# Second attention: who bounds the logarithms of the last two of eight tiles

## The chip, the cores and the metric

The kernel runs on one core of a Trainium2 chip. The metric is the device time of one execution in microseconds (us); lower is better. Engines are named as in the profile: PE is TensorE (PEld its weight loads), DVE is VectorE, ACT is ScalarE, POOL is GpSimd, SP is SyncE.

## The reference, cut to what matters

The whole reference is a chain of a first attention, a mixture-of-experts feed-forward, a second attention and the same feed-forward again, over 4 batches of 1024 tokens of 256 features. The change lies in the second attention, which weighs by inverse squared distance and has no softmax:

```python
sq = q2 + swapaxes(k2, -1, -2) - 2.0 * einsum('bhqd,bhkd->bhqk', Q, K)
dist = sqrt(maximum(sq, 0.0))
W = (SHEP_EPS + dist) ** (-2)
W = W / (SHEP_EPS + sum(W, axis=-1, keepdims=True))
A = einsum('bhqk,bhkd->bhqd', W, V)          # then O = (G * A) @ W_out + X
```

It has 16 heads of 16 features, over two layernorms (the layer's own, and the one in front of it).

## The kernel before, in words

`attention_b` takes the heads in groups of four. Four batches times four groups are 16 units, and each unit is done in two halves of 512 queries: 32 periods, numbered j. In a period the weights are held as `w`, 8 tiles of 128 keys by 4 heads by 512 queries, so one tile (`one(m)`) is 128x2048 f32. Every tile goes through the same steps, each on another engine:

- PE multiplies keys by queries into a ring of three slots (L1951, "dist"); a tile has two slots' worth, one per pair of heads.
- ACT takes the logarithm of both (L1867, in `log`), which writes `w`, and signals `s_log` (L1869). The first time that a tile is rewritten it waits until the old one was used (`s_pv`).
- DVE bounds the logarithm from below by `LOG_MIN`, in place (L1770, in `bound`), and signals `s_bound`.
- ACT takes the sigmoid of minus half of it (L1909), in place, behind a wait on `s_bound`.
- DVE squares it (L1827), in place, and signals `s_wts`.
- PE multiplies values by weights (L1939, "values") into `acc`, and signals `s_pv`.

The sigmoid and the logarithm need different tables, so ACT works in two phases: all eight sigmoids of period j, a table load (L1917), all sixteen logarithms of period j + 1, a table load (L1906). DVE's program follows it: the gates of period j - 1 (L1786 to L1791), eight squares of period j with small work between them, then eight bounds of period j + 1. Each engine has its own queue, written out by hand as a loop over j, and executes it in order; PE's comes from a list (`ORDER`).

The small work of DVE between the squares is, in even periods, the next unit's queries, keys and values (`take`, L1737 to L1744) and their lengths (`lengths`, L1754 and L1757), in odd periods the copies of four transposed operands (`operand`, L1764). Between the bounds, behind bound 3, stands the layernorm of the next batch, three times in a batch: in its second period the first moments (L1708 to L1713), in its third the first normalisation and the second moments, in its fourth the second normalisation (L1723). The last batch has none.

GpSimd has little to do here. In each period it builds two of a unit's four stacks (`build`, L1663 to L1669): in even periods it waits for the lengths, in odd ones for the operand that was copied from the same buffer (`s_qkT`). PE transposes the stacks (L1984), and DVE's `operand` copies them. In the second and third period of a batch it takes the layernorm's root (L1640), and in the third, ahead of that, it makes the next batch's residual with two additions over 128x2048 (L1646 and L1648), as soon as DVE has normalised (`s_x1`). The wait for that is at L1645; the root behind it is needed by DVE one period later.

The change adds a semaphore and a helper to GpSimd, shortens both loops that call `bound` (L1818 and L1838 of the profile's numbering, around `bound(0, m)` and `bound(j + 1, m)`), and changes the wait of the sigmoid at L1908. The functions it touches:

Of the kernel before, what the change touches and what calls it, by code (L numbers as in the profile page):

```python
# [26 lines left out]
TB = L // P  # L27
# [91 lines left out]
def attention_a(nc, c, X, W, sem):  # L119
# [15 lines left out]
    LOWEST = -3.0e38  # L135
    STACKS = [(e, i) for e in range(PAIRS) for i in range(2)]

# [105 lines left out]
    with ExitStack() as ctx:  # L243
# [100 lines left out]
        with nc.Block() as block:  # L344
# [169 lines left out]
            def _(act):  # L514
# [3 lines left out]
                for step in ORDER:  # L518
# [35 lines left out]
                    elif what == "stack":  # L554

                        u, i = step[1:]
                        e, side = STACKS[i]
                        s.copy((kT if side else qT)[:, u % 3, e, :], src).then_inc(s_act, 1)
# [29 lines left out]
            def _(pe):  # L588
                ident = c["ident"]
                pe.wait_ge(s_init, 1)  # L590
                for step in ORDER:
# [37 lines left out]
                    elif what == "stack":  # L629

                        u, i = step[1:]
                        e, side = STACKS[i]
                        pe.wait_ge(s_built, 2 * u + side + 1)
# [855 lines left out]
def attention_b(nc, c, X, x, W, sem):  # L1489
# [7 lines left out]
    UNITS = B * NG  # L1497
    PERIODS = 2 * UNITS
    LOG_MIN = -64.0 * math.log(2.0)
    STACKS = [(e, i) for e in range(PAIRS) for i in range(2)]  # L1500

    def moved(j):
# [5 lines left out]
        if j % 2 and (j + 1) // 2 < UNITS:  # L1508
            out += [("stack", (j + 1) // 2, i) for i in range(len(STACKS))]
        if p == 4 and b + 1 < B:  # L1510
# [5 lines left out]
    def first():  # L1516

        out = [("tokens", 0, x) for x in range(2)] + [("qkv", 0, x) for x in range(2)]
        out += [("stack", 0, i) for i in range(len(STACKS))]
        return out + [("dist", 0, m) for m in range(TB)]  # L1520
# [29 lines left out]
    with ExitStack() as ctx:  # L1550
# [44 lines left out]
        s_qkT = sem("b_stack_transposed")  # L1595
        s_log = sem("b_log_distances")
        s_bound = sem("b_log_distances_bounded")
        s_sig = sem("b_root_weights")
        s_wts = sem("b_weights_ready")
        s_pv = sem("b_weights_used")  # L1600
# [8 lines left out]
        def one(m):  # L1609
            return w[:, m].rearrange("p h n -> p (h n)")  # L1610
# [8 lines left out]
        with nc.Block() as block:  # L1619
# [14 lines left out]
            @block.gpsimd  # L1634
            def _(pool):

                def root(n):

                    pool.wait_ge(s_var, n + 1)
                    pool.tensor_tensor(rstd[:], vpe[:], c["half"][:, 0:TB], ALU.pow).then_inc(s_rstd, 1)  # L1640

                def residual(b):

                    xs = X[:, b * TB:(b + 1) * TB, :]
                    pool.wait_ge(s_x1, b + 1)  # L1645
                    pool.tensor_tensor(xs, xs, xn[:], ALU.add)  # L1646
                    pool.drain()
                    pool.tensor_tensor(xs, xs, b_out[:].unsqueeze(1).to_broadcast([P, TB, D]), ALU.add)  # L1648
                    pool.drain().then_inc(s_xadd, 1)

                def build(n, i):

                    e, side = STACKS[i]
                    heads = slice(2 * e, 2 * e + 2)
                    src = qk[:, :, heads, side, :]
                    norm = len2[:, :, heads, side:side + 1]
                    st = (ks if side else qs)[:].rearrange("p t (h n) -> p t h n", h=2)
                    hi2, lo, at = (DH, 2 * DH, 3 * DH + 2) if side else (2 * DH, DH, 3 * DH)
                    pool.wait_ge(s_len, 2 * n + 2)
                    if n or e:  # L1660

                        pool.wait_ge(s_qkT, len(STACKS) * n + i - 1)
                    pool.tensor_copy(st[:, :, :, 0:DH].bitcast(F32R), src)  # L1663
                    pool.tensor_copy(st[:, :, :, hi2:hi2 + DH].bitcast(F32R), src)
                    pool.tensor_copy(st[:, :, :, at:at + 1].bitcast(F32R), norm)
                    pool.drain()
                    pool.tensor_tensor(st[:, :, :, lo:lo + DH], src, st[:, :, :, 0:DH], ALU.subtract)
                    pool.tensor_tensor(st[:, :, :, at + 1:at + 2], norm, st[:, :, :, at:at + 1], ALU.subtract)
                    pool.drain().then_inc(s_stack, 1)  # L1669

                pool.memset(vg[:], 0.0)
                pool.memset(qs[:], 0.0)
                pool.memset(ks[:], 0.0)
                pool.drain()
                for h in range(2):
                    pool.memset(qs[:, :, h * KC + 3 * DH + 2:h * KC + 3 * DH + 4], 1.0)
                    pool.memset(ks[:, :, h * KC + 3 * DH:h * KC + 3 * DH + 2], 1.0)
                pool.memset(vg[:, :, :, :, DH:DH + 1], 1.0)
                pool.drain().then_inc(s_init, 1)
                root(0)  # L1680
                pool.wait_ge(s_w, WLOADS)
                residual(0)
                root(1)
                for i in range(len(STACKS)):
                    build(0, i)
                for j in range(PERIODS):
                    b, p = divmod(j, TB)
                    n = j // 2 + 1
                    for i in range(2):
                        if n < UNITS:  # L1690
                            build(n, 2 * (j % 2) + i)
                    if b + 1 < B:
                        if p == 1:
                            root(2 * b + 2)
                        if p == 2:
                            residual(b + 1)
                            root(2 * b + 3)

            @block.vector
            def _(dve):  # L1700
# [58 lines left out]
                def operand(n, i):  # L1759

                    at = AT["stack", n, i]
                    e, side = STACKS[i]
                    R.wait_ready(dve, at, ())
                    v.tensor_copy((kT if side else qT)[:, n % 2, e, :], slot(at)).then_inc(R.free[at % SLOTS], 1)  # L1764
                    dve.drain().then_inc(s_qkT, 1)

                def bound(j, m):

                    dve.wait_ge(s_log, TB * j + m + 1)
                    v.tensor_scalar(one(m), one(m), LOG_MIN, None, ALU.max).then_inc(s_bound, 1)  # L1770

# [43 lines left out]
                    lengths(0, x)  # L1815
                for i in range(len(STACKS)):
                    operand(0, i)
                for m in range(TB):  # L1818
                    bound(0, m)
                for j in range(PERIODS):  # L1820
                    b, p = divmod(j, TB)
                    if j:
                        gates(j - 1)
                    n = j // 2 + 1
                    for m in range(TB):
                        dve.wait_ge(s_sig, TB * j + m + 1)
                        v.tensor_tensor(one(m), one(m), one(m), ALU.mult).then_inc(s_wts, 1)  # L1827
                        if n < UNITS:
                            if j % 2 == 0:
                                if m < 2:  # L1830
                                    take(n, m)
                                if m in (4, 5):
                                    lengths(n, m - 4)
                            elif m < len(STACKS):
                                operand(n, m)
                        if b and p < 2 and m == 6:
                            add(b - 1, p)
                    for m in range(TB if j + 1 < PERIODS else 0):  # L1838
                        bound(j + 1, m)
                        if m == 1:  # L1840
                            o_rows(j)
                        if b + 1 < B and m == 3:
                            if p == 1:
                                moments(b + 1, 0)
                            if p == 2:
                                normalise(b + 1, 0)
                                moments(b + 1, 1)
                            if p == 3:
                                normalise(b + 1, 1)
# [7 lines left out]
            def _(act):  # L1857
# [45 lines left out]
                for j in range(PERIODS):  # L1903
                    b, p = divmod(j, TB)
                    n = j // 2 + 1
                    s.preload_act_table_set("sigmoid_and_others")  # L1906
                    for m in range(TB):
                        act.wait_ge(s_bound, TB * j + m + 1)  # L1908
                        s.activation(one(m), one(m), ACT.Sigmoid, scale=-0.5).then_inc(s_sig, 1)  # L1909
                        if j % 2 == 0 and n < UNITS and m in (4, 6):  # L1910
                            squared(n, m // 2 - 2)
                        if p == 4 and b + 1 < B and m in (5, 7):
                            tokens(b + 1, m // 2 - 2)
                        if p < 2 and b and m == 4:
                            turned(b - 1, p)
                    if j + 1 < PERIODS:
                        s.preload_act_table_set("natural_log")  # L1917
                        for m in range(TB):
                            log(j + 1, m)
# [146 lines left out]
```

## Time and profile before

| | us |
|---|---|
| median of 3 runs | 4340.56 |
| lowest and highest run | 4340.33, 4345.66 |
| the profiled execution | 4337.58 |
| its span in the trace | 4335.3 |
| busy in the span: PE, DVE, ACT, POOL | 3583.2, 2565.9, 2235.6, 904.0 |

A row of the profile's groups has line, engine, operation, what it writes and reads, its shape and count; behind the bar the busy time, the mean duration of one in ns, and the idle time of the engine just in front of these instructions with what ended it. "ACTq" is ScalarE's queue: a wait that was ended by its drain, here the signal at L1869. Times in a timeline count from the start of the span. In a timeline consecutive instructions of one line are merged (x4 are four of them), and records of one engine can overlap a little, since the next instruction starts before the last has left the pipeline.

### The profile page before, as it was taken

What the parts mean: (1) busy time and instruction counts of PE and PEld (TensorE: products, weight loads), DVE (VectorE), ACT (ScalarE), POOL (GpSimd) and SP (SyncE); (2) the same over time, 40 slices, a digit from 0 to 9 for tenths busy, and PEclk for the clock granted to TensorE, in tenths of its full rate; (3) what the DMA queues carried; (4) which work ended last, traced back from release to release, by engine and by line L of the source; (5) the groups of instructions that cost most, each with busy time, mean ns of one, the idle gap of its engine ahead of it and who ended that gap; (6) DMA issues with size and microseconds to landing.
All of it is one profiled execution on the core that took longest, in us unless ns stands there. A gap on an engine that the chain in (4) does not pass through costs nothing. (4 is left out here: it accounts for less than half of the span.)

```text
span 4335.3 us, 55982 instructions
## 1 busy us (share of the span) xinstructions
PE 3583.2 (83%) x21924; PEld 2580.9 (60%) x21924; DVE 2565.9 (59%) x3967; ACT 2235.6 (52%) x2873; POOL 904.0 (21%) x882
## 2 busy tenths in 40 slices
PE   2788888897999999994667766766775899999998
PEld 2444444545888899993222332322321688889998
DVE  2556555553443345554988888898888544335554
ACT  1354545554332234442877878878888432224443
POOL 2222222210002201212332232132120001210112
PEclk9799999998999999996867777777777999999999
DMA  3000000001001013422000000000000100102432
GB/s 111 1 1 1 1 1 1 1 1 59 6 22 36 28 65 90 107 66 63 0 1 1 1 1 1 1 1 1 1 1 1 59 11 25 38 17 76 120 84 54
DMA packets 86807, 124.93 MB, mean 29 GB/s; under 512 B 7767, under 2 KB 73257, under 8 KB 86544
## 3 DMA queue, kind: packets, MB, share of 16 engines
q1 hardware_dynamic: 68880, 100.18, 6.8%
q0 software_dynamic: 17664, 21.17, 2.9%
q8 instruction: 174, 2.85, 0.3%
q14 instruction: 89, 0.73, 0.1%
HBM read 85.15 MB, written 42.55 MB: 29 GB/s over the span
## 5 line engine op out<-in xcount | busy, mean ns | idle before, releaser
L1827 DVE TENSOR_TENSOR b_w<-b_w 128x2048 f32<-128x2048 f32 x256 | 585.2, 2317 | 36.8 <-ACT b_w L1909 28.2
L472 DVE TENSOR_REDUCE a_mxp<-a_deep 128x1 f32<-128x512 f32 (+3 forms) x768 | 392.2, 552 | 355.3 <-PE a_deep L652 294.3
L1867 ACT ACTIVATE b_w<-b_ring 128x1024 f32<-128x1024 f32 x512 | 496.5, 1022 | 174.9 <-PE b_ring L1951 143.1
L1939 PE MATMUL b_acc<-b_w,b_vg 128*32 128x512 f32 x2048 | 331.0, 731 | 182.9 <-DVE b_w L1827 182.6
L1909 ACT ACTIVATE b_w<-b_w 128x2048 f32<-128x2048 f32 x256 | 468.0, 1897 | 1.4
L1381 ACT ACTIVATE f1hid<-f1ring 128x512 f32<-128x512 f32 (+2 forms) x256 | 132.6, 518 | 577.6 <-PE f1ring L1461 560.5
L1381 ACT ACTIVATE f2hid<-f2ring 128x512 f32<-128x512 f32 (+2 forms) x256 | 132.6, 518 | 576.6 <-PE f2ring L1461 559.6
L571 ACT ACTIVATE a_prob<-a_wide 128x1024 f32<-128x1024 f32 (+1 forms) x320 | 294.2, 943 | 239.2 <-PE a_wide L682 164.9
L1299 DVE TENSOR_TENSOR f1hid<-f1hid,f1ring 128x512 f32<-128x512 f32 (+2 forms) x256 | 150.2, 587 | 440.2 <-ACT f1hid L1381 440.1
L1299 DVE TENSOR_TENSOR f2hid<-f2hid,f2ring 128x512 f32<-128x512 f32 (+2 forms) x256 | 150.2, 587 | 438.6 <-ACT f2hid L1381 438.5
L1951 PE MATMUL b_ring<-b_qT,b_kT 64*128 64x512 f32 x1024 | 278.1, 573 | 142.0 <-ACT b_w L1867 121.2
L1770 DVE TENSOR_SCALAR b_w<-b_w 128x2048 f32<-128x2048 f32 x256 | 326.4, 1292 | 101.1 <-ACTq L1869 100.4
L1461 PE MATMUL f2ring<-f2xh,f2wg 128*128 128x512 f32 (+2 forms) x1536 | 326.1, 354 | 10.8 <-DVE f2xh L1282 8.6
L1461 PE MATMUL f1ring<-f1xh,f1wg 128*128 128x512 f32 (+2 forms) x1536 | 326.1, 354 | 10.5 <-DVE f1xh L1282 8.3
L1951 PEld LDWEIGHTS b_ring<-b_qT,b_kT 64*128 64x128 f32 x1024 | 106.2, 218 | 379.2 <-ACT b_w L1867 262.7
L1461 PEld LDWEIGHTS f1ring<-f1xh,f1wg 128*128 128x128 f32 x1536 | 250.8, 190 | 35.5 <-DVE f1xh L1282 9.2
L1461 PEld LDWEIGHTS f2ring<-f2xh,f2wg 128*128 128x128 f32 x1536 | 250.6, 190 | 35.7 <-DVE f2xh L1282 9.5
L648 PE MATMUL a_deep<-a_kT,a_qT 64*128 64x512 f32 (+3 forms) x768 | 175.2, 453 | 89.4 <-DVE a_mxp L472 88.5
L1663 POOL CAST b_qs<-b_qk 128x256 fp32r<-128x256 f32 x32 | 74.1, 2315 | 818.9 <-DVE b_len L1757 643.1
L1939 PEld LDWEIGHTS b_acc<-b_w,b_vg 128*32 128x32 f32 x2048 | 45.3, 117 | 331.6 <-DVE b_w L1827 291.4
L1480 PEld LDWEIGHTS f1acc<-f1wd,f1hh 128*128 128x128 f32 x1536 | 200.7, 191 | 17.0 <-DVE f1hh L1127 7.6
L1480 PEld LDWEIGHTS f2acc<-f2wd,f2hh 128*128 128x128 f32 x1536 | 200.7, 191 | 17.1 <-DVE f2hh L1127 7.6
(348 smaller groups left out, 6816.8 us busy)
## 6 DMA issues: line engine op xcount, KB each, us to landing
X<-expert_in SPq DMA_DIRECT2D x16, 650.0 KB, 4.8
expert_in<-zeros SPq DMA_DIRECT2D x8, 650.0 KB, 8.0
X<-in_x SPq DMA_DIRECT2D x4, 1024.0 KB, 9.6
x_mid<-X SPq DMA_DIRECT2D x8, 512.0 KB, 3.2
f1raw_x<-in_rd SPq DMA_DIRECT2D x4, 1024.0 KB, 5.3
f1raw_xf<-in_rg SPq DMA_DIRECT2D x4, 1024.0 KB, 5.1
f1raw_xf<-in_ru SPq DMA_DIRECT2D x4, 1024.0 KB, 7.2
f1raw_g<-in_rg SPq DMA_DIRECT2D x4, 1024.0 KB, 4.9
```

Source lines behind the costliest of these rows:

```text
L472: v.tensor_reduce(mxp[:, t, 2 * e + h, i:i + 1], dslot(step, h)[:, 0:n], AX_X, ALU.max).then_inc(s_dve, 1)
L571: s.activation(dst, src.rearrange("p (h e n) -> p h e n", h=2, e=pairs)[:, :, :, 0:n], ACT.Exp).then_inc(s_act, 1)
L1299: v.tensor_tensor(hid[:, s % 2, 0:n], hid[:, s % 2, 0:n], slot(step)[:, QC:QC + n], ALU.mult).then_inc(free_of(step), 1)
L1381: s_eng.activation(hid[:, s % 2, 0:n], slot(step)[:, 0:n], ACT.Silu).then_inc(s_silu, 1)
L1461: last = pe.matmul(dst[:, j * QC:j * QC + n], w[:, a, cc, i * P:(i + 1) * P], xh[:, b, x, cc, first:first + n], start=(k == 0 and cc == 0) ...
L1480: last = pe.matmul(acc[:, g % 2, t * D:(t + 1) * D], hh[:, s % 2, a, t * P:(t + 1) * P], w[:, part, i, :], start=(i == 0 and k == 0 and t ...
L1770: v.tensor_scalar(one(m), one(m), LOG_MIN, None, ALU.max).then_inc(s_bound, 1)
L1827: v.tensor_tensor(one(m), one(m), one(m), ALU.mult).then_inc(s_wts, 1)
L1867: s.activation(w[:, m, 2 * pair:2 * pair + 2, :].rearrange("p h n -> p (h n)"), slot(at + pair), ACT.Ln, scale=SHEP_EPS ** -2).then_inc(R. ...
L1909: s.activation(one(m), one(m), ACT.Sigmoid, scale=-0.5).then_inc(s_sig, 1)
L1939: last = pe.matmul(acc[32 * h:32 * h + 32, qc, :], vg[:, u % 2, h, x, :], w[:, x, h, :], start=(x == 0), stop=(x == TB - 1))
L1951: last = pe.matmul(slot(n + e)[:, h * QC:(h + 1) * QC], kT[at, u % 2, e, x * P:(x + 1) * P], qT[at, u % 2, e, qc * QC:(qc + 1) * QC], star ...
```

## The change

The bounds of tiles 6 and 7 of every period are taken by GpSimd (the same maximum, the same operand) and signalled by a semaphore of their own. In GpSimd's program they stand behind the period's builds and in front of its root and residual. DVE keeps tiles 0 to 5.

```diff
+    ON_DVE = TB - 2
+    ON_POOL = TB - ON_DVE
...
+        s_late = sem("b_last_log_distances_bounded")
...
+                def late_bound(j, m):
+
+                    pool.wait_ge(s_log, TB * j + m + 1)
+                    pool.tensor_scalar(one(m), one(m), LOG_MIN, None, ALU.max).then_inc(s_late, 1)
...
                 for i in range(len(STACKS)):
                     build(0, i)
+                for m in range(ON_DVE, TB):
+                    late_bound(0, m)
                 for j in range(PERIODS):
                     b, p = divmod(j, TB)
                     n = j // 2 + 1
                     for i in range(2):
                         if n < UNITS:
                             build(n, 2 * (j % 2) + i)
+                    for m in range(ON_DVE, TB if j + 1 < PERIODS else ON_DVE):
+                        late_bound(j + 1, m)
                     if b + 1 < B:
                         if p == 1:
                             root(2 * b + 2)
...
-                for m in range(TB):
+                for m in range(ON_DVE):
                     bound(0, m)
...
-                    for m in range(TB if j + 1 < PERIODS else 0):
+                    for m in range(ON_DVE if j + 1 < PERIODS else 0):
                         bound(j + 1, m)
...
-                        act.wait_ge(s_bound, TB * j + m + 1)
+                        if m < ON_DVE:
+                            act.wait_ge(s_bound, ON_DVE * j + m + 1)
+                        else:
+                            act.wait_ge(s_late, ON_POOL * j + m - ON_DVE + 1)
                         s.activation(one(m), one(m), ACT.Sigmoid, scale=-0.5).then_inc(s_sig, 1)
```

## Rows read from the trace of the kernel before

**Rows 1.** The page's first part: busy time, share of the span, instructions.

```profile
PE 3583.2 (83%) x21924; PEld 2580.9 (60%) x21924; DVE 2565.9 (59%) x3967; ACT 2235.6 (52%) x2873; POOL 904.0 (21%) x882
```

**Rows 2.** Groups of instructions between 2040 and 3355 us.

```profile
L1827 DVE TENSOR_TENSOR b_w<-b_w 128x2048 f32<-128x2048 f32 x256 | 585.2, 2317 | 36.8 <-ACT b_w L1909 28.2 <-issue 0.5
L1867 ACT ACTIVATE b_w<-b_ring 128x1024 f32<-128x1024 f32 x512 | 496.5, 1022 | 174.9 <-PE b_ring L1951 143.1 <-issue 30.8
...
L1770 DVE TENSOR_SCALAR b_w<-b_w 128x2048 f32<-128x2048 f32 x256 | 326.4, 1292 | 101.1 <-ACTq L1869 100.4
```

**Rows 3.** Single lines: ns min/median/max, first and last start, and releasers.

```profile
L1770 DVE TENSOR_SCALAR b_w<-b_w x256: 1208/1227/5568, 2041.0 to 3333.4; 128x2048 f32<-128x2048 f32 x128
...
  ACTq L1869: 100.4, 127
...
  ACT b_w L1909: 28.2, 32
...
L1640 POOL TENSOR_TENSOR b_rstd<-b_vpe,half x8: 1646/3228/3367, 1992.8 to 2850.0; 128x8 f32<-128x8 f32 x8
```

**Rows 4.** Timeline of DVE, an ordinary period end: start, us, line.

```profile
2303.26 1.23 DVE L1770 TENSOR_SCALAR b_w<-b_w 128x2048 f32<-128x2048 f32 x1 [0.88 <-ACTq L1869]
2305.36 1.23 DVE L1770 TENSOR_SCALAR b_w<-b_w 128x2048 f32<-128x2048 f32 x1 [0.88 <-ACTq L1869]
...
2307.44 0.42 DVE L1791 TENSOR_TENSOR b_gated<-b_gate,b_den 128x256 f32<-128x256 f32 x1
2308.63 2.29 DVE L1827 TENSOR_TENSOR b_w<-b_w 128x2048 f32<-128x2048 f32 x1 [0.77 <-ACT b_w L1909]
```

**Rows 5.** Timeline of ACT, the same end.

```profile
2303.36 1.94 ACT L1867 ACTIVATE b_w<-b_ring 128x1024 f32<-128x1024 f32 x2 [0.17 <-issue]
2305.39 1.28 ACT L1906 ACT_TABLE_LOAD   x1
2306.69 3.71 ACT L1909 ACTIVATE b_w<-b_w 128x2048 f32<-128x2048 f32 x2
```

**Rows 6.** Timeline of DVE, the end with a residual.

```profile
2174.23 8.97 DVE L1770 TENSOR_SCALAR b_w<-b_w 128x2048 f32<-128x2048 f32 x4
...
2184.03 0.43 DVE L1791 TENSOR_TENSOR b_gated<-b_gate,b_den 128x256 f32<-128x256 f32 x1
2184.38 2.29 DVE L1827 TENSOR_TENSOR b_w<-b_w 128x2048 f32<-128x2048 f32 x1
```

**Rows 7.** Timeline of ACT, the same end.

```profile
2171.64 1.94 ACT L1867 ACTIVATE b_w<-b_ring 128x1024 f32<-128x1024 f32 x2 [0.17 <-issue]
```

**Rows 8.** Timeline of DVE, an end behind first moments.

```profile
2131.85 4.67 DVE L1770 TENSOR_SCALAR b_w<-b_w 128x2048 f32<-128x2048 f32 x4
```

**Rows 9.** Timeline of POOL, the end with a residual.

```profile
2169.73 4.56 POOL L1646 TENSOR_TENSOR X<-X,b_xn 128x2048 f32<-128x2048 f32 x1 [1.30 <-DVEq L1725]
2174.44 5.40 POOL L1648 TENSOR_TENSOR X<-X,b_b_out 128x2048 f32<-128x2048 f32 x1
2180.02 3.23 POOL L1640 TENSOR_TENSOR b_rstd<-b_vpe,half 128x8 f32<-128x8 f32 x1 [0.18 <-issue]
2187.98 2.50 POOL L1663 CAST b_qs<-b_qk 128x256 fp32r<-128x256 f32 x1 [4.73 <-DVEq L1765]
```

**Rows 10.** Groups of POOL over the whole span, by form.

```profile
L406 POOL TENSOR_TENSOR X<-X,a_bo 128x2048 f32<-128x2048 f32 x4 | 18.3, 4586 | 0.7 <-issue 0.7
...
L338 POOL CAST a_ks<-a_qk 128x512 fp32r<-128x512 f32 x15 | 9.2, 614 | 0.0
...
L1665 POOL CAST b_ks<-b_len 128x16 fp32r<-128x16 f32 x32 | 6.9, 214 | 0.0
...
L79 POOL TENSOR_SCALAR a_tmp<-a_tmp 128x64 f32<-128x64 f32 x16 | 3.9, 244 | 2.6 <-issue 2.6
```

**Rows 11.** Timeline of PE, the ordinary end.

```profile
2303.33 1.08 PE L1991 MATMUL b_ring<-ident,b_oT 128*128 128x128 f32 x4 [0.21 <-ACT b_w L1867]
```

## The prediction

> **What bounds the kernel now.** I read the page's first part, then the groups of the second attention alone, then the order of time around one end of a period. The page shows no engine at its limit over the whole span [rows 1]; the change touches only the stretch from 2040 to 3355 us, so that stretch decides. There VectorE's squares (L1827), ScalarE's logarithms (L1867) and VectorE's bounds (L1770) are the costly groups [rows 2]. The bounds look like a prize: 64 of the 256 leave VectorE, 64 x 1.227 us [rows 3] = 78.5 us. So the question is which of them sits on the path.
>
> VectorE sat idle before bounds for 100.4 us, 127 times, for the logarithms; before squares it waited for ScalarE's sigmoid 32 times, 28.2 us in all [rows 3], once in a period. Both say that in the log phase ScalarE leads. An ordinary period end shows why. A tile's two logarithms come every 2.11 us and a bound takes 1.23 [rows 4, 5], so VectorE rests between bounds. The last logarithm ends at 2305.30. Then ScalarE loads its table (1.28) and takes sigmoid 0 until 2308.60; the first square starts at 2308.63 [rows 4, 5]. Meanwhile VectorE does bound 7 (to 2306.59) and the gates (to 2307.86), and idles 0.77 us. Bound 6 ends before bound 7's logarithm does. Neither bound 6 nor 7 is on the path; table load plus sigmoid is. From a first square to the next logarithm phase nothing of the bounds takes part.
>
> Three ends differ, one in each of the first three batches: the ones in which VectorE also normalises the next batch. Here the last logarithm ends at 2173.58, but the first square starts at 2184.38, 10.80 us later in place of 3.33, and VectorE's records lie end to end between [rows 6, 7]. The four bounds 4 to 7 took 8.97 us [rows 6]; where nothing stops them four take 4.67 [rows 8], so 4.3 is a stall. Its owner is GpSimd's residual: its second addition starts at 2174.44, in the middle of bound 4, gets going when that bound ends at 2175.45, and ends at 2179.84 [rows 9]; VectorE's next bound has one record of some 5.56 us, as the maximum of its line says [rows 3]. So VectorE and GpSimd exclude each other here, whole instruction by whole instruction, and the one that was waiting goes next.
>
> **The change, part by part.**
>
> Removed from VectorE: 29 ordinary period ends lose two bounds each. Gain 0: cover is table load plus sigmoid 0, 3.3 us after the last logarithm [rows 5].
>
> Added on GpSimd: 64 maxima over 128x2048 f32. No row has this operation at this size. Its casts, with one input as here, took 0.214 us for 16 elements and 0.614 for 512: 0.81 ns an element, so about 0.20 + 2048 x 0.81 ns = 1.86; the only tensor_scalar, 0.244 us for 64 elements, lies on that line (0.25) [rows 10]. I take 1.9 us, since operation and input count agree. Lower bound 1.22, VectorE's own [rows 3]; upper bound 4.59, the two-input sum of the same size [rows 10].
>
> The Trainium skill speaks against this edit: "Trainium Architecture — The Big Picture", in "The five engines, in one table", calls GpSimd unfit for streaming elementwise work, two times slower than VectorE. Twice VectorE's row would be 2.45 us rather than 1.9; no run yet shows which, and it is a rival below.
>
> Ordinary end with 1.9: maximum 6 starts 0.1 after the seventh tile's logarithms and ends 0.1 before the eighth's; maximum 7 runs from 0.1 to 2.0 us after them. VectorE is free there: bound 5 ended long before. The transposes that the gates read start at 2303.33 and take 1.08 [rows 11], so the gates begin before the last logarithm ends; only their final product (two SBUF inputs, 0.42) can be shut out, and it then ends at 2.5 us. The first square is due at 3.33. Cost 0, slack 0.8. Sigmoids 6 and 7 come 10 us later. In reverse, each stage tolerates up to about 2.35 us a maximum: two of them from 2.0 us before the last logarithm, plus the product, make 3.33.
>
> Layernorm's first half (three ends): bounds 4 to 7 run together from 2131.85, 1.15 apart [rows 8]. Bound 5 now ends at 2134.2, the maximum 6, asked for at 2133.2, gets in after it, maximum 7 ends at 2138.1 to 2138.5, and the first square is due at 2138.56. GpSimd's root, queued behind, has passed among bounds without stopping them (3.23 us from 2180.02, nothing added to the bounds) [rows 6, 9]. I take +0.1 each, bounds 0 and 0.5.
>
> The residual ends (three). In GpSimd's program the residual and the second root stand behind both maxima, so the residual's first addition, which now lies under statistics that it does not disturb (2169.73 to 2174.29), moves behind the last logarithm. On the trace's clock: maximum 6 from 2171.6 to 2173.5; bound 4 to 2174.7; maximum 7 to 2176.6; bound 5 to 2177.7; first addition (4.42 once it has the port) to 2182.1; gate product to 2182.5; second addition to 2187.0; first square to 2189.2. It ended at 2186.67 [rows 6]. So two bounds saved, 2.3, and one addition's and one maximum's stall added: +2.5 us. If maximum 7 goes before bound 4 the same pieces add up to the same 2189.2. What is late next: the cast behind that square releases GpSimd's stack build (2187.98) [rows 9], whose transposes VectorE waits for, so the delay is passed on whole. Bounds: 0, were GpSimd's additions to fit gaps, and +4.4, a whole addition more.
>
> Sum: 29 x 0 + 3 x 0.1 + 3 x 2.5 = +8 us. The profiled execution took 4337.58 us (span 4335.3), so it becomes 4345.6; the median, 3 us above it, becomes 4348.6.
>
> **Rivals.** A measurement here can tell about 0.2%, 8.7 us, from no change.
>
> Forecast, +8 us, 4348.6: the port's turns in three ends. Chance 0.60; its own range 4344 to 4354.
>
> GpSimd slower than I think (slower, 0.18). It decides from 2.35 us a maximum: the first square of every period then waits for maximum 7. By VectorE's doubled row, 2.45: maximum 7 ends 3.0 us after the logarithms, the product at 3.4, +0.1 for 29 ends = 3, and 3 x 2 x 0.55 = 3 more: 4355. At the two-input rate, 4.49: maximum 7 ends at 7.1, the square waits until 7.5, 29 x 4.2 = 122, plus 3 x 7.6 = 23: 4486. For it: the skill's two-times rule; against it: the casts' line with the tensor_scalar on it.
>
> VectorE wins the port whenever both wait (faster, 0.12). Then bounds 4 and 5 and the gates are done by 2177.1, the first square starts at 2177.2, and the build waits for GpSimd alone: 2173.6 + 1.9 + 4.4 + 4.4 + 1.65 for the root [rows 3] = 2186.0 at best against 2187.98: -2 x 3 = -6 us, 4334.6. For it: VectorE's queue is never empty here. Against: at 2175.4 the waiting addition went first.
>
> No change (0.10): the first square of the three ends is late but the wait for the stacks, further on, swallows it: 4340.6. Against: that wait starts from the same square.
>
> **How the numbers follow.** The likeliest gives 4348.6. The range, 4334 to 4362, holds forecast, no change, the faster rival and the milder half of the slower one. Within 0.2%: 0.38 of the forecast's 0.60 (its sum lies just inside 8.7), nearly all of no change, 0.08 of the faster rival, together 0.55; slower by more: 0.22 + 0.17 = 0.39; faster by more: 0.06.
>
> **What would show it.** Right: GpSimd's maxima near 1.9 us; in ordinary ends the first square still 3.33 us after the last logarithm; in three ends 13.3 in place of 10.80, with both additions behind the logarithms and one long record of a gate product and one of a square; VectorE less busy by some 78 us without profit. Wrong: maxima over 2.35 us with VectorE's squares waiting in every period; or the three ends shorter than 10.80, which would say that the port's turns are not what I read; or a time that moved where no first square did.

## The result, and the profile after

| | us |
|---|---|
| median before, same session | 4340.44 |
| median after, 4 runs (lowest, highest) | 4429.39 (4425.15, 4431.22) |
| ratio, with its 95% interval | 1.0203 (1.0185 to 1.0221) |
| the profiled execution and its span | 4425.15, 4423.4 |
| busy in the span: PE, DVE, ACT, POOL | 3591.2, 2628.9, 2235.8, 1282.2 |

The change costs 89 us. The forecast was +8, with a range up to 4362, so it is far off. The line numbers of the changed kernel: GpSimd's maximum is L1677, VectorE's bound L1782, its square L1839, the gates L1798 to L1803, ScalarE's logarithm L1879 and sigmoid L1924.

First the groups of the second attention in the changed kernel (the stretch ends 90 us later), to set beside [rows 2].

```profile
L1839 DVE TENSOR_TENSOR b_w<-b_w 128x2048 f32<-128x2048 f32 x256 | 661.8, 2615 | 55.5 <-ACT b_w L1924 47.3
...
L1677 POOL TENSOR_SCALAR b_w<-b_w 128x2048 f32<-128x2048 f32 x64 | 405.2, 6341 | 479.2 <-ACTq L1881 479.2
...
L1782 DVE TENSOR_SCALAR b_w<-b_w 128x2048 f32<-128x2048 f32 x192 | 256.1, 1353 | 54.9 <-ACTq L1881 54.4
```

VectorE was relieved of 64 bounds, and yet its busy time in the whole span rose from 2565.9 to 2628.9 us: the squares alone grew from 585.2 to 661.8, their mean from 2317 to 2615 ns. The line of the squares alone, before and after, with the shortest, the median and the longest of them in ns:

```profile
L1827 DVE TENSOR_TENSOR b_w<-b_w x256: 2280/2287/2798, 2058.6 to 3352.1; 128x2048 f32<-128x2048 f32 x128
```

```profile
L1839 DVE TENSOR_TENSOR b_w<-b_w x256: 2273/2286/6594, 2058.5 to 3442.0; 128x2048 f32<-128x2048 f32 x128
```

The shortest and the median are what they were, so the long ones did not compute for longer; they stood waiting inside their own records. The gates' last product, 0.42 us in [rows 4], has long records too (1.83 us in the ordinary end below). What runs beside them is GpSimd's maximum, with a mean of 6.3 us where I had counted 1.9.

The line of the maximum alone shows what part of that is the operation and what part waiting.

```profile
L1677 POOL TENSOR_SCALAR b_w<-b_w x64: 5354/6054/7497, 2053.3 to 3423.2; 128x2048 f32<-128x2048 f32 x64
```

The shortest is 5.354 us. The two tiles of an ordinary end mostly take 5.36 and 7.49 us.

Now the timeline of an ordinary end, the one that answers to [rows 4, 5]: VectorE, then GpSimd, then ScalarE.

```profile
2319.26 1.23 DVE L1782 TENSOR_SCALAR b_w<-b_w 128x2048 f32<-128x2048 f32 x1 [0.88 <-ACTq L1881]
...
2323.50 1.83 DVE L1803 TENSOR_TENSOR b_gated<-b_gate,b_den 128x256 f32<-128x256 f32 x1
2326.73 2.29 DVE L1839 TENSOR_TENSOR b_w<-b_w 128x2048 f32<-128x2048 f32 x1 [1.41 <-ACT b_w L1924]
2328.94 0.68 DVE L1749 TENSOR_TENSOR b_qk<-b_ring,b_b_in 128x512 f32<-128x512 f32 x1
...
2330.21 4.46 DVE L1839 TENSOR_TENSOR b_w<-b_w 128x2048 f32<-128x2048 f32 x1
```

```profile
2321.42 12.82 POOL L1677 TENSOR_SCALAR b_w<-b_w 128x2048 f32<-128x2048 f32 x2 [23.77 <-ACTq L1881]
```

```profile
2321.46 1.94 ACT L1879 ACTIVATE b_w<-b_ring 128x1024 f32<-128x1024 f32 x2 [0.17 <-issue]
2323.50 1.28 ACT L1918 ACT_TABLE_LOAD   x1
```

The last logarithm ends at 2323.40 and the first square starts at 2326.73, so 3.33 us later, exactly as before. The loss is one square further on. GpSimd's first maximum (2321.42) lasts its 5.36 us until 2326.78. The gates' product waits for it (1.83 us in place of 0.42), at no cost, but square 0 does not, although the maximum ends 0.05 us later than the square begins. The second maximum then waits for square 0 to end at 2329.02; then it has the port, until 2334.24. Square 1 (2330.21) has a record of 4.46 us in place of 2.29: it waited for 2.17 of them. The same happens in 28 of the 29 ordinary ends; in the other, the first behind a residual, the second maximum came 0.2 us ahead of square 0, and that one waited (5.55 us). Measured from the last logarithm, square 4 mostly ends at 19.13 us in place of 16.96 in an even period and at about 24.5 in place of 22.4 in an odd one; in the last two periods, where nothing stands between squares, at 17.87 in place of 14.43. 27 x 2.15 + 2 x 3.44 = 65 us. GpSimd's late bounds themselves kept nobody waiting: ScalarE's sigmoids stood idle for 0.9 us in all, for bounds of VectorE.

The rest is in the three ends with a residual, here the one of [rows 6] and [rows 9].

```profile
2179.02 3.73 DVE L1725 TENSOR_SCALAR b_vpe<-b_mv 128x8 f32<-128x8 f32 x1
2180.93 9.16 DVE L1782 TENSOR_SCALAR b_w<-b_w 128x2048 f32<-128x2048 f32 x2
...
2190.92 3.83 DVE L1803 TENSOR_TENSOR b_gated<-b_gate,b_den 128x256 f32<-128x256 f32 x1
2194.68 6.59 DVE L1839 TENSOR_TENSOR b_w<-b_w 128x2048 f32<-128x2048 f32 x1
```

```profile
2177.35 11.66 POOL L1677 TENSOR_SCALAR b_w<-b_w 128x2048 f32<-128x2048 f32 x2 [3.15 <-ACTq L1881]
2189.00 5.47 POOL L1649 TENSOR_TENSOR X<-X,b_xn 128x2048 f32<-128x2048 f32 x1
2194.62 4.51 POOL L1651 TENSOR_TENSOR X<-X,b_b_out 128x2048 f32<-128x2048 f32 x1
2199.30 3.50 POOL L1643 TENSOR_TENSOR b_rstd<-b_vpe,half 128x8 f32<-128x8 f32 x1 [0.18 <-issue]
```

```profile
2177.40 1.94 ACT L1879 ACTIVATE b_w<-b_ring 128x1024 f32<-128x1024 f32 x2 [0.17 <-issue]
```

The last logarithm ends at 2179.34. GpSimd works almost without a gap from 2177.35 to 2202.80: two maxima, two additions, the root. VectorE goes in between, one instruction at a time: the last step of its statistics (3.73 us, with eight elements a partition; 0.23 where nothing stops it), two bounds in 9.16 us, one product of the gates in 3.83, square 0 in 6.59. Square 0 ends 21.93 us after the last logarithm; before it was 13.09, so 8.8 us less. In the third of these ends the second addition stops square 1 and not square 0. From first logarithm to first logarithm the three periods sum to 171.5 us in place of 145.3, 26 more, and 65 + 26 = 91, of the 90 that the second attention is longer from its first logarithm to its last square (1405.4 against 1315.4). The rest of the kernel takes 3018.0 us in place of 3019.9, so the whole loss lies in this stretch.

### The profile page after: what moved, and what is told of

The parts are those of the page before. It is cut to its first block and busy times, and to the rows that moved or that the text cites. A ratio compares the mean times of both kernels' runs of the same rounds, so it can differ in the third digit from the quotient of the medians.

```text
span 4423.4 us, 55982 instructions
## 1 busy us (share of the span) xinstructions
PE 3591.2 (81%) x21924; PEld 2582.9 (58%) x21924; DVE 2628.9 (59%) x3903; ACT 2235.8 (51%) x2873; POOL 1282.2 (29%) x946
## 5 line engine op out<-in xcount | busy, mean ns | idle before, releaser
L1839 DVE TENSOR_TENSOR b_w<-b_w 128x2048 f32<-128x2048 f32 x256 | 661.8, 2615 | 55.5 <-ACT b_w L1924 47.3
L1879 ACT ACTIVATE b_w<-b_ring 128x1024 f32<-128x1024 f32 x512 | 496.5, 1022 | 221.5 <-PE b_ring L1966 191.3
L1677 POOL TENSOR_SCALAR b_w<-b_w 128x2048 f32<-128x2048 f32 x64 | 405.2, 6341 | 479.2 <-ACTq L1881 479.2
L1924 ACT ACTIVATE b_w<-b_w 128x2048 f32<-128x2048 f32 x256 | 468.3, 1897 | 2.2 <-DVE b_w L1782 0.9
L1782 DVE TENSOR_SCALAR b_w<-b_w 128x2048 f32<-128x2048 f32 x192 | 256.1, 1353 | 54.9 <-ACTq L1881 54.4
```

The lines of the kernel that those rows point to most:

```text
L1677: pool.tensor_scalar(one(m), one(m), LOG_MIN, None, ALU.max).then_inc(s_late, 1)
L1879: s.activation(w[:, m, 2 * pair:2 * pair + 2, :].rearrange("p h n -> p (h n)"), slot(at + pair), ACT.Ln, scale=SHEP_EPS ** -2).then_inc(R. ...
```

## The experiments

All are compared with the kernel before, run in between on the same chip. Its median there was 4343 to 4345 us, so differences are best read from the ratios.

**What a GpSimd instruction costs by itself.** A list of instructions in front of the second attention, three times each; the drains between them are left out here, and the comments give the profile's lines.

```diff
+                flat = vg[:].rearrange("p a h t d -> p (a h t d)")   # 128x2048
+                for _ in range(3):
+                    pool.tensor_scalar(flat, flat, LOG_MIN, None, ALU.max)            # L1675
+                    pool.tensor_scalar(flat[:, 0:512], ..., LOG_MIN, None, ALU.max)   # L1677
+                    pool.tensor_scalar(flat[:, 0:64], ..., LOG_MIN, None, ALU.max)    # L1679
+                    pool.tensor_scalar(flat, flat, 0.0, None, ALU.add)                # L1681
+                    pool.tensor_scalar(flat, flat, 1.0, None, ALU.mult)               # L1683
+                    pool.tensor_scalar(flat, flat, 1.0, None, ALU.min)                # L1685
+                    pool.tensor_scalar(flat, flat, 1.0, 0.0, ALU.mult, ALU.add)       # L1687
+                    pool.tensor_scalar(flat[:, 0:64], ..., 1.0, 0.0, ALU.mult, ALU.add)  # L1689
+                    pool.tensor_copy(flat, flat)                                      # L1691
+                    pool.tensor_tensor(flat, flat, flat, ALU.add)                     # L1693
```

> A list of single GpSimd instructions in front of the second attention, three times each, while nothing needs their results; the time of the kernel is of no interest. Theory A, the price is the maximum's own (a comparison is dear on GpSimd): the 2048-wide tensor_scalar with max and with min takes 5.3 us, with add and mult about 1.9. Theory B, the price is that of any one-input arithmetic of GpSimd, and only copies are cheap: add, mult, max, min all about 5.3, the copy 1.9. Theory C, the price comes from what ran beside it in the attention: all of them about 1.9 here, max too. The 64-wide and 512-wide ones say whether it grows straight with the size (0.25 and 1.4 us under A and B for max).

```profile
L1683 POOL TENSOR_SCALAR b_vg<-b_vg 128x2048 f32<-128x2048 f32 x3 | 16.2, 5384 | 0.5 <-issue 0.5
...
L1675 POOL TENSOR_SCALAR b_vg<-b_vg 128x2048 f32<-128x2048 f32 x3 | 16.1, 5371 | 0.8 <-issue 0.8
...
L1687 POOL TENSOR_SCALAR b_vg<-b_vg 128x2048 f32<-128x2048 f32 x3 | 5.7, 1897 | 0.5 <-issue 0.5
L1691 POOL COPY b_vg<-b_vg 128x2048 f32<-128x2048 f32 x3 | 5.7, 1889 | 0.4 <-issue 0.2
...
L1677 POOL TENSOR_SCALAR b_vg<-b_vg 128x512 f32<-128x512 f32 x3 | 4.5, 1483 | 0.5 <-issue 0.5
...
L1679 POOL TENSOR_SCALAR b_vg<-b_vg 128x64 f32<-128x64 f32 x3 | 1.1, 363 | 0.5 <-issue 0.5
...
L1689 POOL TENSOR_SCALAR b_vg<-b_vg 128x64 f32<-128x64 f32 x3 | 0.7, 242 | 0.5 <-issue 0.5
```

The maximum takes 5.37 us with nothing beside it (its start and that of the next lie 5.5 us apart, the drain between them included, so the length of the record can be trusted), so the price is its own and theory C falls. Multiplication costs the same, and so do addition (5.377) and minimum (5.360, neither shown), so A falls too. The copy takes 1.89: B holds, with one exception that matters here. (The last of the list, an addition of the tile to itself, took 3.60, also less than the maximum.) The tensor_scalar with two operations, multiply then add, takes 1.90 us for 2048 elements and 0.242 for 64. That is the very form of the one tensor_scalar in the trace before [rows 10], on which the estimate rested. The maximum of 64 takes 0.363, of 512 1.483: 2.5 to 2.6 ns an element, where the casts have 0.81.

**Are two operations the key?** The bound as max-max would compute the same and might be as fast.

```diff
-                    pool.tensor_scalar(one(m), one(m), LOG_MIN, None, ALU.max).then_inc(s_late, 1)
+                    pool.tensor_scalar(one(m), one(m), LOG_MIN, LOG_MIN, ALU.max, ALU.max).then_inc(s_late, 1)
```

> The changed kernel with GpSimd's maximum written in two stages (max with the bound, then max with the bound again; the result is the same). Theory: a GpSimd tensor_scalar of one stage goes at 2.6 ns an element and one of two stages at 0.83, whatever the operations, so the maxima take 1.9 us, the 29 ordinary ends lose nothing, the three residual ends about 2 us each, 4343 to 4350 us. Rival: only multiply-then-add is fast in two stages and the maximum stays at 5.4 or becomes dearer: 4430 or more.

4471.18 us, ratio 1.0297 (1.0281 to 1.0313): dearer, not cheaper. The shortest maximum took 7.068 us. A second list settled which pairs.

```diff
+                    pool.tensor_scalar(flat, flat, LOG_MIN, LOG_MIN, ALU.max, ALU.max)   # L1675
+                    pool.tensor_scalar(flat, flat, LOG_MIN, 0.0, ALU.max, ALU.add)       # L1677
+                    pool.tensor_scalar(flat, flat, 0.0, 0.0, ALU.add, ALU.add)           # L1679
+                    pool.tensor_scalar(flat[:, 0:512], ..., LOG_MIN, LOG_MIN, ALU.max, ALU.max)  # L1681
+                    pool.tensor_scalar(w[:, 0].rearrange(...), flat, LOG_MIN, None, ALU.max)     # L1683
+                    pool.tensor_scalar(flat[:, 0:1024], ..., LOG_MIN, None, ALU.max)             # L1685
```

> A second list of single GpSimd tensor_scalars in front of the second attention, three times each. Theory: two stages go at 0.83 ns an element whatever the operations, 1.9 us for max-max, max-add and add-add of 2048, 0.6 for max-max of 512; one stage goes at 2.6 ns an element, 2.8 us for 1024, and the same 5.4 for 2048 when it writes another tile than it reads. Rival: only some pairs are fast; or it is writing in place that is slow, and the one that writes elsewhere takes 1.9.

```profile
L1679 POOL TENSOR_SCALAR b_vg<-b_vg 128x2048 f32<-128x2048 f32 x3 | 21.3, 7107 | 0.5 <-issue 0.5
L1675 POOL TENSOR_SCALAR b_vg<-b_vg 128x2048 f32<-128x2048 f32 x3 | 21.3, 7090 | 0.5 <-issue 0.5
L1677 POOL TENSOR_SCALAR b_vg<-b_vg 128x2048 f32<-128x2048 f32 x3 | 21.3, 7085 | 0.5 <-issue 0.5
L1683 POOL TENSOR_SCALAR b_w<-b_vg 128x2048 f32<-128x2048 f32 x3 | 16.1, 5359 | 0.8 <-issue 0.8
L1685 POOL TENSOR_SCALAR b_vg<-b_vg 128x1024 f32<-128x1024 f32 x3 | 8.3, 2763 | 0.5 <-issue 0.5
L1681 POOL TENSOR_SCALAR b_vg<-b_vg 128x512 f32<-128x512 f32 x3 | 5.8, 1929 | 0.5 <-issue 0.5
```

My theory fell, and its rival holds: of the pairs tried only multiply-add is fast; the others take 7.1 us. That the maximum writes where it reads makes no difference (5.36 into another tile). I found no form of the bound at 1.9 us. The dearer maximum is of use as a larger dose of the same, though: in the ordinary ends of even periods square 4 ends at 19.99 us, 3.03 later than before, against 2.17 with the 5.36 us form.

**The same places with a cheap instruction.** This asks whether the price was the only fault. The bounds of tiles 6 and 7 are left out here, and a copy of the tile onto itself stands in their place.

```diff
-                    pool.tensor_scalar(one(m), one(m), LOG_MIN, None, ALU.max).then_inc(s_late, 1)
+                    pool.tensor_copy(one(m), one(m)).then_inc(s_late, 1)
```

> The changed kernel with the maximum on GpSimd replaced by a copy of the tile onto itself (the bound of tiles 6 and 7 is left out), so same places, same waits, an instruction that should take 1.9 us. Port-turn theory (VectorE and GpSimd exclude each other instruction by instruction, and only the place of GpSimd's time matters): as in the prediction, first squares 3.33 us after the last logarithm in the 29 ordinary ends, 2.5 us more in the three residual ends, 4348 us. Rival (each us of GpSimd work takes a fixed share from VectorE, wherever it lies: 89 us for 405 us of maxima): about 4340 + 0.22 x 122 = 4367.

4343.64 us, ratio 1.0001 (0.9991 to 1.0010). In the ordinary ends square 0 starts 3.33 us after the last logarithm and square 4 ends where it did before (16.96 us in the even periods). In the first of the three residual ends:

```profile
2165.86 4.05 DVE L1782 TENSOR_SCALAR b_w<-b_w 128x2048 f32<-128x2048 f32 x2
...
2170.73 3.83 DVE L1803 TENSOR_TENSOR b_gated<-b_gate,b_den 128x256 f32<-128x256 f32 x1
2174.49 6.63 DVE L1839 TENSOR_TENSOR b_w<-b_w 128x2048 f32<-128x2048 f32 x1
```

```profile
2164.02 1.90 POOL L1677 COPY b_w<-b_w 128x2048 f32<-128x2048 f32 x1 [3.12 <-ACTq L1881]
2166.13 2.70 POOL L1677 COPY b_w<-b_w 128x2048 f32<-128x2048 f32 x1 [0.21 <-ACTq L1881]
2168.79 5.49 POOL L1649 TENSOR_TENSOR X<-X,b_xn 128x2048 f32<-128x2048 f32 x1
2174.43 4.54 POOL L1651 TENSOR_TENSOR X<-X,b_b_out 128x2048 f32<-128x2048 f32 x1
```

```profile
2164.09 1.94 ACT L1879 ACTIVATE b_w<-b_ring 128x1024 f32<-128x1024 f32 x2 [0.17 <-issue]
```

The last logarithm ends at 2166.03 and square 0 at 2181.12, 15.09 us later, 2.0 more than before. The forecast's order of turns is there piece by piece: a copy, a bound, a copy, a bound, an addition, the gates' product (3.83), an addition, square 0 (6.63). Its size, 2.5, was 0.5 too large. The three residual periods sum to 150.9 us in place of 145.3, 5.5 more; the whole second attention is 3.4 us longer. The median shows nothing of it: the interval of its ratio ends at 1.0010, which is 4 us. The rival with a fixed share (4367) is out.

**Only one of the two tiles on GpSimd.** The same maximum, half as many, in two places.

```diff
-    ON_DVE = TB - 2
-    ON_POOL = TB - ON_DVE
+    LATE = (6,)            # e_only6; (7,) in e_only7, (5, 7) in e_5and7, (2,) in e_only2
+    EARLY = tuple(m for m in range(TB) if m not in LATE)
...
-                    for m in range(ON_DVE, TB if j + 1 < PERIODS else ON_DVE):
+                    for m in (LATE if j + 1 < PERIODS else ()):
                         late_bound(j + 1, m)
...
```

> Only tile 6 goes to GpSimd, tile 7 stays on VectorE. Port-turn theory: the maximum of tile 6 runs from 0.1 us behind its logarithm for 5.36 us, so until 3.3 us after the last one; VectorE's bound 7 is shut out until then and ends at 4.4, the gates at 5.8, the first square starts there in place of 3.33: +2.4 in 29 ends = 70, and about 5 in each of three = 15: 4425. Rival (fixed share): half of the loss, 4385. Second rival (only the second of the two maxima costs, as it alone met a square in the changed kernel): 4341 to 4356.

> Only tile 7 goes to GpSimd. Port-turn theory: its maximum takes the port 0.1 us after the last logarithm and keeps it until 5.46; the gates' product is shut out until then, the first square starts at 5.9 in place of 3.33: +2.6 in 29 ends = 75, and about 6 in each of three = 18: 4433, as dear as both tiles together. Rival (fixed share): half of the loss, 4385.

Tile 6 alone: 4426.62 us, ratio 1.0185 (1.0168 to 1.0202). Tile 7 alone: 4376.2, ratio 1.0073 (1.0057 to 1.0090). Half of the work costs nearly all of the loss in one place and a third in the other, so no fixed share holds. The first forecast was right (4425; the first square of most ordinary ends starts at 5.62 us, with 5.8 expected), the second was not (4433): with tile 7 alone the three residual periods are 20 us longer, near the 18 forecast, but the 29 ordinary ends together only some 13 in place of 75. The timelines of both, VectorE and GpSimd, show why; first tile 6.

```profile
2320.88 1.23 DVE L1782 TENSOR_SCALAR b_w<-b_w 128x2048 f32<-128x2048 f32 x1 [0.88 <-ACTq L1881]
2325.09 4.38 DVE L1782 TENSOR_SCALAR b_w<-b_w 128x2048 f32<-128x2048 f32 x1 [2.99 <-ACTq L1881]
...
2330.65 2.29 DVE L1839 TENSOR_TENSOR b_w<-b_w 128x2048 f32<-128x2048 f32 x1
```

```profile
2323.04 5.36 POOL L1677 TENSOR_SCALAR b_w<-b_w 128x2048 f32<-128x2048 f32 x1 [23.77 <-ACTq L1881]
```

Bound 7, asked for at 2325.09, ends at 2329.47, 1.07 us after the maximum (2328.40), so it really began at about the maximum's end. A bound is shut out for the maximum's whole length. Now tile 7.

```profile
2317.21 0.42 DVE L1803 TENSOR_TENSOR b_gated<-b_gate,b_den 128x256 f32<-128x256 f32 x1
2320.45 2.82 DVE L1839 TENSOR_TENSOR b_w<-b_w 128x2048 f32<-128x2048 f32 x1 [2.81 <-ACT b_w L1924]
```

```profile
2317.23 5.62 POOL L1677 TENSOR_SCALAR b_w<-b_w 128x2048 f32<-128x2048 f32 x1 [26.06 <-ACTq L1881]
```

The gates' product came 0.02 us ahead of the maximum and was not stopped, as in most ordinary ends; in seven of the 29 it came behind, waited, and the first square started at 3.95 us. The maximum then had the port from about 2317.63 and ended at 2322.85, but square 0, asked for at 2320.45, took only 0.53 us more than its 2.29. So a square may start 3.35 us after a maximum has got the port, long before it ends. The changed kernel says the same: port at 2329.02, square 1 free at 2332.38, 3.36 us. I had taken both kinds of stall for the same. It is no chance of these two ends: in the changed kernel 57 squares and products of the gates were stopped by a maximum, and each, counted back from the end of its record, got going 1.87 or 1.88 us before the maximum ended; with max-max it was 2.73 us before, all 57 times. Behind GpSimd's additions in these kernels, and behind the copies of the run above, it was 0.14 or 0.15 us before the end, so those shut products and squares out for practically their whole length.

**Two tests of the refined rule.** A maximum shuts bounds out for all of its 5.3 us and squares (and the gates' product) for the first 3.4.

> GpSimd takes the bounds of tiles 5 and 7 in place of 6 and 7: the same 64 maxima of 5.36 us. Refined port-turn theory (a GpSimd maximum shuts VectorE's bounds out for all of its 5.3 us, and VectorE's products of two tiles for its first 3.4): maximum 5 runs until 1.3 us after the last logarithm, bound 6 behind it ends at 2.4, maximum 7 holds off the gates' product until 5.7 and runs to 7.6, the first square starts at 6.1 in place of 3.33: +2.8 in 29 ends = 80, about 8.5 in each of three = 26: 4449. Rival (fixed share of 405 us of maxima): as the changed kernel, 4430.

4447.48 us, ratio 1.0243 (1.0226 to 1.0260), with 4449 expected. The first squares of most ordinary ends start at 6.02 us, with 6.1 expected, against 3.33 in the changed kernel: the same 64 maxima, one of the two moved by a tile, cost some 18 us more. In its parts the total was luckier than the rule: the three ends behind first moments start at 9.81, which I had not foreseen (the last step of the statistics, 0.17 us in the kernel before, has a record of 4.99 there, under maximum 5), and the three residual periods sum to 165.6 us, 20 longer than before and not 26.

> Only tile 2 goes to GpSimd, all others stay on VectorE. Refined port-turn theory: in the ends behind odd periods GpSimd is free when the logarithm of tile 2 is done, holds VectorE's bounds off for 5.3 us early in the logarithm phase, and VectorE makes it up before the last bound: first square at 3.33, nothing lost. In the ends behind even periods GpSimd still builds stacks until about 5 us before the last logarithm, its maximum falls on bounds 5 to 7, first square at about 5.0: 13 x 1.7 = 22; three residual ends at 5 each = 15: 4380. Rival (fixed share): half of the changed kernel's loss in every end, odd or even, 1.1 us each, 4385.

4374.6 us, ratio 1.0073 (1.0056 to 1.0090), with 4380 expected. The ends divide, if less cleanly than I wrote. Behind odd periods ten first squares of 16 stay at 3.33 us; the six with layernorm work between VectorE's bounds start at 4.6 to 5.9 instead; that the slack was spent on that work is my reading. Behind even periods six of 13 start at 4.5 to 4.7 (5.0 expected), the others at 3.3 to 3.7. The three residual periods together are 16 us longer (15 expected). In the free ends GpSimd works 5.36 us and nothing is lost, since VectorE makes up the delay before its last bound. The total alone would not decide against a fixed share (4385); ends that lose nothing do.

**What the two bounds are worth to VectorE.** They are left out altogether, and nothing is added on GpSimd.

```diff
-                for m in range(ON_DVE, TB):
-                    late_bound(0, m)
...
-                            act.wait_ge(s_late, ON_POOL * j + m - ON_DVE + 1)
+                            act.wait_ge(s_log, TB * j + m + 1)
```

> The bounds of tiles 6 and 7 left out altogether (their sigmoids wait for the logarithm): 78 us less on VectorE, nothing added on GpSimd. Port-turn theory: 29 ends unchanged, since table load and sigmoid set them; in the three residual ends two bounds fewer on the path, 2.3 us each: 4336. Rival (VectorE's load counts everywhere): up to 78 us less, 4265.

4332.18 us, ratio 0.9976 (0.9967 to 0.9986). VectorE is busy 2491.4 us, 74.5 less, and the kernel gains some 10. The three residual periods, from first logarithm to first logarithm, sum to 138.0 us in place of 145.3: 7.3, the 2.3 each that was expected. The ordinary ends are unchanged at 3.33. So even a second engine that cost nothing could have brought no more than these 10 us.

**The stall that was there already.** The residual's second addition moves to where VectorE has slack; all bounds stay on VectorE. The kernel computes all that it did.

```diff
                     pool.tensor_tensor(xs, xs, xn[:], ALU.add)
-                    pool.drain()
+                    pool.drain().then_inc(s_xadd, 1)
+
+                def biased(b):
+
+                    xs = X[:, b * TB:(b + 1) * TB, :]
                     pool.tensor_tensor(xs, xs, b_out[:].unsqueeze(1).to_broadcast([P, TB, D]), ALU.add)
-                    pool.drain().then_inc(s_xadd, 1)
+                    pool.drain().then_inc(s_biased, 1)
...
                 residual(0)
+                biased(0)
...
+                        if p == 5:
+                            pool.wait_ge(s_log, TB * (j + 1) + 3)
+                            biased(b + 1)
...
+                    dve.wait_ge(s_biased, b + 1)      # in add(b, x)
```

> The kernel before with the second addition of the residual (the bias, 4.5 us of GpSimd) moved from the residual ends into the logarithm phase three periods later, behind the logarithm of tile 2, where VectorE has slack; all bounds on VectorE. Port-turn theory: the three residual ends lose their 4.4 us stall, first square 6.4 in place of 10.8 us after the last logarithm, nothing elsewhere: 13 us less, 4330. Rival: the stall only moves to the new place or to the build of the stacks behind it: 4343.

4326.75 us, ratio 0.9971 (0.9961 to 0.9982): faster than both kernels, by some 12 us against the one before. VectorE and GpSimd at the same end:

```profile
2171.23 1.06 DVE L1722 TENSOR_SCALAR b_vpe<-b_mv 128x8 f32<-128x8 f32 x1
2172.20 4.63 DVE L1779 TENSOR_SCALAR b_w<-b_w 128x2048 f32<-128x2048 f32 x4
...
2178.00 2.28 DVE L1837 TENSOR_TENSOR b_w<-b_w 128x2048 f32<-128x2048 f32 x1
```

```profile
2167.72 4.54 POOL L1647 TENSOR_TENSOR X<-X,b_xn 128x2048 f32<-128x2048 f32 x1 [1.30 <-DVEq L1734]
2172.43 3.30 POOL L1641 TENSOR_TENSOR b_rstd<-b_vpe,half 128x8 f32<-128x8 f32 x1 [0.18 <-DVE b_vpe L1722]
```

The four bounds take 4.63 us in place of 8.97, and the first square starts 6.45 us after the last logarithm (2171.56) in place of 10.80. The three periods sum to 132.1 us, 13.2 less than before, and the other ends keep their 3.33.

## Why the prediction was wrong, and where it was right

**What bounds the kernel:** right. Table load and sigmoid 0 set the ordinary end, before and after; bounds 6 and 7 are worth nothing there and 2.3 us in the three residual ends, which leaving them out showed.

**The price of the maximum:** this is the step that failed, the term of 1.9 us for one maximum. "About 0.20 + 2048 x 0.81 ns = 1.86 ... I take 1.9 us": it took 5.36. The line was drawn through casts, and the one tensor_scalar of the trace lay on it, but that one multiplies and adds, and of all forms tried this is the only one with the casts' rate. I looked at its name and size and not at its operations. With 64 elements, besides, the two rates differ by 0.12 us only (0.242 against 0.363). The upper bound, 4.59 us from a two-input sum, was no bound either: one input is not always cheaper than two. The range stopped at 4362, short even of the 4486 that this bound gave.

The Trainium skill's "Trainium Architecture — The Big Picture", in "The five engines, in one table", which warned of this with a factor of two, was nearer than my row but still mild: 5.36 against 1.227 us is a factor of 4.4 for this operation. By the factor of two the time would have been 4355.

**The ordinary ends:** the threshold of 2.35 us a maximum was passed, so the rival's place was right and its size wrong. By its working 5.36 us would have cost more than 4.2 us an end; it cost 2.15. Two things were missing. The second maximum comes after square 0 has begun, waits for it, and so strikes square 1. And a square is shut out for 3.4 us and not for the whole of the maximum, which tile 7 alone showed.

**The residual ends:** right in their mechanism. The residual falls behind both maxima, its first addition stops the gates' product and its second stops square 0. With an instruction of 1.9 us square 0 ended 2.0 us later in place of 2.5; with the real one 8.8. Two pieces of the working were off without harm. "One addition's and one maximum's stall" against two bounds saved would be 4.4 + 1.9 - 2.3 = 4.0 us, not 2.5; the 2.5 comes from the order of turns written out, in which bound 4 starts 0.7 us earlier than before and most of the gates lie under the first addition, as they did with the copy. And the statistics were not all undisturbed by the first addition: their last step takes 1.07 us beside it in the kernel before and 0.23 with the copy, which is why bound 4 can start earlier.

**Within what can be measured:** with the copy the kernel stands at 1.0001 (0.9991 to 1.0010). So for the instruction that I thought it was, the range and the mechanism would have held; the +8 us (1.0018) would still have been too much.

## What to carry to other kernels

Before work is moved to an engine that takes turns with the one it comes from, measure that instruction there by itself, in its exact form: same operations, same count of them, same size. Then lay the two engines' instructions along one clock: what counts is which instruction of the critical engine meets a long one of the other, and the same 5.4 us cost between nothing and more than two microseconds depending on the tile. And where an engine waits inside its records, its busy time rises: a mean above the minimum of the same line is a wait to be looked for, and here the older one, the residual's, was worth more than the change.

## What the runs showed of the hardware

GpSimd's tensor_scalar on 128x2048 f32 took 5.36 to 5.38 us with one operation (max, min, add or mult), 7.09 to 7.11 with max-max, max-add and add-add, and 1.90 with mult-add, as much as a copy (1.89). Why that pair differs was not found.

VectorE and GpSimd took turns instruction by instruction. A bound of VectorE (one input and one output, both in SBUF, 1.23 us for 2048) waited for the end of GpSimd's maximum, and so did a one-input tensor_scalar of eight elements (3.73 us in place of 0.23). A square or a product (two inputs in SBUF) waited only 3.35 us of the maximum's 5.2, and 4.2 of max-max's 6.9, but nearly the whole of an addition's 4.4. The Trainium skill's "SBUF — State Buffer", in "Who interferes with whom", says of a VectorE instruction in a two-port mode that whoever issues first has the shared pair for the whole instruction. For the bounds the traces agree (4.38 us in place of 1.23), though no row names the mode in which a bound runs. Of an instruction with two SBUF inputs the same section of the Trainium skill says that it contends with a GpSimd instruction that reads SBUF, and not for how long; by these traces that depends on GpSimd's instruction. How a GpSimd instruction reads and writes over its length was not looked at, so the reason is open.
